# Packed diagonal maxima, exponent floors on ScalarE and unread transposes at the end of a fused attention and FP4 layer

## The chip, the cores and the metric

The kernel runs on one core of a Trainium2 chip. The metric is the device time of one execution in microseconds. The engines are PE (TensorE), DVE (VectorE), ACT (ScalarE), POOL (GpSimd) and SP (SyncE, which only issues transfers here).

## What is computed

One block adds two branches to its input of 2048 rows of 128. `_layernorm` takes away the mean and divides by the deviation.

```python
x = L0_attn_hidden_states                      # (1, 2048, 128)
xn = _layernorm(x, axis=-1)
x = x + _L0_attn_ref(xn, w_attn, b_attn, w_proj, b_proj) + _L0_ffn_ref(xn, w_gate, w_up, w_down)
...
# attention: 16 heads of 8
scores = jnp.einsum('bhqd,bhkd->bhqk', q, k) * scaling
scores = scores + _power_law_mask(S, scores.dtype)[None, None]   # -log(distance + 1), one side only
attn = jax.nn.softmax(scores, axis=-1)
out = jnp.einsum('bhqk,bhkd->bhqd', attn, v)
...
# FFN, inner width 352; every operand is first put through blocks of 16 on the FP4 grid
scale = jnp.maximum(jnp.max(jnp.abs(xb), axis=-1, keepdims=True) / 6.0, 1e-12)
q = _GRID[jnp.searchsorted(_MID, jnp.abs(xb / scale))] * jnp.sign(xb / scale) * scale
h = jax.nn.silu(fp4_linear(x, w_gate)) * fp4_linear(x, w_up)
return fp4_linear(h, w_down)
```

A query sees the keys from its own place on, so only one triangle of the 2048 x 2048 scores is used.

## The kernel before

**Units.** The attention works in 16 units: four groups of 512 queries (`GROUPS`, in the order 3, 2, 0, 1) by four sets of four heads. Each unit has two parts.

**Maxima.** First come the row maxima. For each of four blocks of 128 queries (`a`), each of four heads (`j`) and each group of 512 keys (`c`) from the unit's own on, PE multiplies queries by keys into one bank of PSUM (L1354). For the unit's own group (`c == g`) only the 512 - 128a keys from the block's own on are needed, and a second matmul adds the triangular mask (L1357). DVE then takes the maximum of the bank's columns into one column of `mxp` (L1135). Two closing reduces over `mxp` (item `parts`, L1146 and L1151) make the negated maxima, POOL splits them into three bfloat16 parts (item `minor`), PE turns them (item `rows`), and a transfer sets them into rows of `qop`, so that the next product subtracts them by itself.

**Steps.** Then come the steps, 160 over all units, each one block of 128 keys for the four heads. PE multiplies keys by queries (item `st`, L1378, with the mask at L1381 on the diagonal), ACT takes the exponential (L954), the result is multiplied by the distance weights, and PE multiplies by the values (item `pv`, L1396, one step is four matmuls in the program and eight records in the trace). Weighing is done for two heads at once by POOL (L802) from a ring of eight slots, or for one head by DVE straight from PSUM (L1162). After a unit's last step ACT copies the sums (item `evac`, L979), PE turns them (`close`, L1404), DVE divides (`norm`), and after four units PE turns the result (`turn`, L1412), ACT adds a bias (L973) and PE projects (`project`, L1419).

**FFN.** Sixteen tiles of 128 rows run beside this. PE makes gate and up (item `gu`), ACT copies and makes the curves (`curve`, L922 to L931), DVE works through the nine `silu` stages (L1097 to L1121): the product, the maximum of each block of 16, the scale, the scaled values, and then the rounding unit. That is the exponent's bits by themselves (L1117) and `max(e, 1) * ROUND` (L1121). POOL rounds by adding and taking away this unit and multiplies by the scale (item `quant`, L818, L820, L822), PE turns the tile (`hT`) and multiplies it by the down weights (`down`). The input and the weights go through the same rounding early, in six pieces (item `fp4`, L1041 to L1058 on DVE, then L782 to L789 on POOL).

**Order.** `plan()` simulates the engines with costs of its own and writes each engine's list of items; `build()` issues them in that order, so on the chip each engine's order is fixed. On PE a `max` item has rank 4 while DVE has fewer than two of them ahead and rank 7 after that, `st` has 4.5. On DVE a `max` item has rank 4 while the maxima are behind a curve of needed lead, and otherwise 7, behind the weighing at 5. The planner gives a pair of heads to DVE where POOL's queue is behind by more than a limit:

```python
behind = max(clock["POOL"], now) + waiting["POOL"] - now
pair_vec[p] = behind > (LAST_QUEUE if work["max"] == total else POOL_QUEUE)
```

The first limit, 1500, holds once all the maxima are done, 3800 before. `FILL` items of PE, transposes into a bank that nobody reads (L1244), stand early in the program.

## Time and profile before

| | |
|---|---|
| median of 3 runs | 627.31 us (627.09 to 627.82) |
| the profiled execution's own time | 626.35 us |
| its span in the profile | 624.5 us |
| busy: PE, DVE, ACT, POOL | 564.4, 562.8, 400.8, 537.4 us |
| share of the span | 90%, 90%, 64%, 86% |

The span runs from the first instruction to the last; some microseconds of the execution lie outside it. A matmul's end is modelled, so PE's busy time holds the time that a result needs to come out of the array. An engine's busy time counts overlapping instructions once.

### The profile page before, as it was taken

How to read it: one execution, taken by the hardware profiler on the slowest of the kernel's cores; microseconds unless marked ns; L12 is line 12 of the kernel's file. 1: busy time of each engine (PE TensorE's matmuls, PEld its weight loads, DVE VectorE, ACT ScalarE, POOL GpSimd, SP SyncE). 2: the span in 40 equal slices, each digit the busy share in tenths (PEclk: the TensorE clock that was granted, in tenths of full speed). 3: DMA queues.
4: the chain of work that ended last, by engine and by line, in shares of the span. 5: the costliest groups of instructions: out<-in, count | busy, mean ns of one | idle time of the engine just before them, and what ended most of it. 6: DMA issues, size and time to landing. Idle time of an engine off the chain costs nothing.

```text
span 624.5 us, 11270 instructions
## 1 busy us (share of the span) xinstructions
PE 564.4 (90%) x3807; PEld 250.9 (40%) x3807; DVE 562.8 (90%) x1178; ACT 400.8 (64%) x857; POOL 537.4 (86%) x400
## 2 busy tenths in 40 slices
PE   6999779999999999999989899999989898989985
PEld 5576534444343334333333332342334242432322
DVE  6899998989999999999999999998989999997661
ACT  4576457566656475767667577666656667759782
POOL 7226987789899989999998999999998999998992
PEclk9999988999999999999999999999999999999997
DMA  5255341310000000200000000000000000000000
GB/s 148 74 137 114 119 83 51 78 43 36 2 2 3 0 2 10 86 1 2 2 0 2 19 1 1 2 2 1 1 2 1 19 0 2 1 2 1 1 2 17
DMA packets 14715, 16.66 MB, mean 27 GB/s; under 512 B 1594, under 2 KB 14171, under 8 KB 14243
## 3 DMA queue, kind: packets, MB, share of 16 engines
q1 hardware_dynamic: 14123, 15.70, 9.2%
q8 instruction: 30, 0.49, 0.3%
q10 hardware_dynamic: 536, 0.26, 0.2%
q14 instruction: 26, 0.21, 0.1%
HBM read 11.75 MB, written 4.01 MB: 25 GB/s over the span
## 4 chain that ended last, share of the span: by engine, by line
PE 43%; POOL 32%; DVE 13%; ACT 7%; issue 4%; ACTq 0%; POOLq 0%; DVEq 0%
POOL ring L802 25%; PE psum L1396 11%; PE psum L1354 9%; PE psum L1378 7%; DVE mxp L1135 7%; ACT ring L954 2%; POOL xw L820 2%; POOL xw L818 2%; PE psum L1331 2%; POOL xw L822 2%; PE psum L1312 2%; PE psum L1314 1%; PE psum L1320 1%; DVE ring L1162 1%; PE psum L1404 1%
## 5 line engine op out<-in xcount | busy, mean ns | idle before, releaser
L802 POOL TENSOR_TENSOR ring<-ring,dist 128x1024 f32<-128x1024 f32 (+3 forms) x223 | 438.4, 1996 | 31.7 <-ACT ring L954 31.3
L1135 DVE TENSOR_REDUCE mxp<-psum 128x1 f32<-128x512 f32 (+3 forms) x640 | 352.6, 598 | 20.5 <-PE psum L1354 11.4
L954 ACT ACTIVATE ring<-psum 128x512 f32<-128x512 f32 (+3 forms) x446 | 211.5, 528 | 101.5 <-PE psum L1381 51.9
L1354 PE MATMUL psum<-kop,qop 96*128 96x512 bf16 (+3 forms) x640 | 198.0, 352 | 7.3 <-DVE mxp L1135 5.3
L1378 PE MATMUL psum<-qop,kop 128*128 128x512 bf16 (+3 forms) x640 | 190.7, 349 | 6.2 <-DVE mxp L1135 3.7
L1396 PE MATMUL psum<-ring,vaug 128*32 128x512 f32 (+3 forms) x1280 | 151.5, 544 | 15.0 <-POOL ring L802 14.1
L1162 DVE TENSOR_TENSOR ring<-psum,dist 128x512 f32<-128x512 f32 (+3 forms) x194 | 115.7, 622 | 13.9 <-ACT psum L954 13.8
L954 ACT ACTIVATE psum<-psum 128x512 f32<-128x512 f32 (+3 forms) x194 | 99.5, 543 | 39.7 <-PE psum L1378 23.4
L1354 PEld LDWEIGHTS psum<-kop,qop 96*128 96x128 bf16 x640 | 57.2, 97 | 127.8 <-DVE mxp L1135 46.5
L1378 PEld LDWEIGHTS psum<-qop,kop 128*128 128x128 bf16 x640 | 59.7, 97 | 82.2 <-DVE mxp L1135 15.5
L1357 PE MATMUL psum<-tri_q,identb 128*128 128x128 bf16 x256 | 56.2, 221 | 0.0
L1381 PE MATMUL psum<-tri_k,identb 128*128 128x128 bf16 x256 | 52.3, 219 | 0.0
L1396 PEld LDWEIGHTS psum<-ring,vaug 128*32 128x32 f32 x1280 | 26.7, 108 | 61.0 <-issue 59.9
L1357 PEld LDWEIGHTS psum<-tri_q,identb 128*128 128x128 bf16 x256 | 25.2, 99 | 12.2 <-issue 1.1
L1244 PE MATMUL psum<-identf 128*128 128x128 f32 x200 | 29.9, 274 | 0.0
L1381 PEld LDWEIGHTS psum<-tri_k,identb 128*128 128x128 bf16 x256 | 25.1, 98 | 7.9 <-issue 0.3
L1244 PEld LDWEIGHTS psum<-identf 128*128 128x128 f32 x200 | 22.1, 141 | 2.0 <-issue 0.5
L922 ACT ACTIVATE xw<-psum 128x352 f32<-128x352 f32 x16 | 7.4, 464 | 22.4 <-PE psum L1314 22.4
L807 POOL TENSOR_TENSOR mres<-mneg,mpart 128x16 f32<-128x16 f32 x16 | 3.6, 227 | 20.4 <-DVE mpart L1151 20.4
L782 POOL TENSOR_TENSOR xw<-xw,hT 128x512 f32<-128x512 f32 (+1 forms) x6 | 7.8, 1304 | 10.4 <-DVE hT L1058 10.4
L1331 PE MATMUL psum<-wdT,hT 128*128 128x128 f32 (+1 forms) x96 | 14.9, 291 | 1.4 <-ACT hT L940 1.2
L820 POOL TENSOR_TENSOR xw<-xw 128x352 f32<-128x352 f32 x16 | 14.9, 931 | 1.3
(130 smaller groups left out, 490.2 us busy)
## 6 DMA issues: line engine op xcount, KB each, us to landing
kop<-parts_dram SPq DMA_DIRECT2D x9, 384.0 KB
qop<-parts_dram SPq DMA_DIRECT2D x9, 384.0 KB
parts_dram<-qpart SPq DMA_DIRECT2D x18, 128.0 KB, 2.8
xin<-_attn_hidden_states_dram SPq DMA_DIRECT2D x4, 256.0 KB, 4.7
ring<-inv_dram SPq DMA_DIRECT2D x1, 1024.0 KB, 4.9
out_dram<-xin SPq DMA_DIRECT2D x4, 256.0 KB, 2.3
parts_dram<-qpart SPq DMA_DIRECT2D x6, 96.0 KB
qop<-parts_dram SPq DMA_DIRECT2D x3, 192.0 KB
```

The lines of the kernel that those rows point to most:

```text
L802: g_.tensor_tensor(slot(p)[:, :, 0:n], slot(p)[:, :, 0:n], both, ALU.mult).then_inc(weighed_pool, 1)
L820: g_.tensor_tensor(v, v, c, ALU.subtract).then_inc(hq_seq, 1)
L954: a_.activation(scores if pair_vec[p] else slot(p)[:, e % 2, 0:n], scores, ACT.Exp, scale=SCALE).then_inc(exp_done, 1)
L1135: v_.tensor_reduce(mxp[:, u % 2, 4 * a + j, c - g:c - g + 1], bank(*o)[:, 0:n], AX_X, ALU.max).then_inc(max_used, 1)
L1162: v_.tensor_tensor(slot(p)[:, e % 2, 0:n], bank("st", e)[:, 0:n], weights(d, n), ALU.mult).then_inc(weighed_vec, 1)
L1244: nc.tensor.transpose(psum[:, OUT_BANK, 0:P], identf[:], identf[:])
L1331: ins = mm(down_of(i), hT[0:k, i % 2, m], wdT[0:k, m], start=(m == 0), stop=(m == 2))
L1354: ins = mm(bank(*o)[:, 0:n], qop[0:K_MAX, u // NQ % 2, h, P * a:P * (a + 1)], kop[0:K_MAX, h, k0:k0 + n], start=True, stop=(c != g))
L1357: ins = mm(bank(*o)[:, 0:P], identb[:], tri_q[:], start=False, stop=True)
L1378: ins = mm(bank(*o)[:, 0:n], kop[0:K_ST, h, P * b:P * (b + 1)], qop[0:K_ST, u // NQ % 2, h, 0:n], start=True, stop=(d >= TPG))
L1381: ins = mm(bank(*o)[:, P * d:P * (d + 1)], identb[:], tri_k[:], start=False, stop=True)
L1396: ins = mm(psum[32 * j:32 * j + 32, OUT_BANK, 0:n], vaug[:, b, VC * h:VC * h + 32], slot(2 * s + j // 2)[:, j % 2, 0:n], start=(b == NT - ...
```

## The change

**Packed maxima.** In a unit's own key group, the bank of block 0 stays as it was. Block 1 (384 keys) and block 3 (128 keys) of one head now share a bank, and block 2 (256 keys) of two heads share one. One DVE reduce takes four maxima of 128 columns each from such a bank. Over a unit that is 10 banks in place of 16; the matmuls are the same in number and columns, each with its mask. `mxp` has three more columns per row (`NMX`), and its rows stand in the order 0, 2, 1, 3 (`ROW_OF`), so that four results lie side by side. The closing reduces read all seven columns, and where the next unit but one has fewer key groups, a memset clears the last of them.

**Floors on ACT.** `max(e, 1) * ROUND` becomes `Relu(ROUND * e - ROUND) + ROUND`: two passes of ACT with bias operands from `rounds`, for the 16 tiles (item `floor`) and the six pieces (item `floor4`). DVE has a stage fewer in both, and POOL waits for ACT in place of DVE.

**Unread transposes.** After the last `pv` PE may take 24 `tail` items, transposes of the identity into a free bank, at the lowest rank.

```diff
-SILU_STAGES, FP4_STAGES = 9, 6
+SILU_STAGES, FP4_STAGES = 8, 5
+NMX = NG + 3
+ROW_OF = [0, 2, 1, 3]
+TAIL = 24
...
+def max_pieces(a, j):
+    if a == 1:
+        return [(1, j), (3, j)]
+    if a == 2:
+        return [(2, j), (2, j + 1)] if j % 2 == 0 else []
+    return [(0, j)] if a == 0 else []
...
+    for k in range(TAIL):
+        pe(("tail", k), 2 * P, [], rank=9)
...
+        act(("floor4", n), GQ, [("DVE", ("fp4", n, FP4_STAGES - 1))], n=2, rank=3)
...
-                    pe(item, n + (P if c == g else 0), needs, rank=6)
-                    vec(item, n, [("PE", item)], rank=6)
+                    pe(item, GQ + (P * len(pieces) if c == g else 0), needs, rank=6)
+                    vec(item, GQ, [("PE", item)], rank=6)
...
-        pool(("quant", i), 2700, [("DVE", ("silu", i, SILU_STAGES - 1))], rank=0)
+        act(("floor", i), F, [("DVE", ("silu", i, SILU_STAGES - 1))], n=2, rank=2)
+        pool(("quant", i), 2700, [("ACT", ("floor", i))], rank=0)
...
+            if kind == "tail" and ("PE", ("pv", len(steps) - 1)) not in seen:
+                return None
...
-            work["max"] += TPG - item[2] if item[4] == units[item[1]][0] else TPG
+            work["max"] += TPG
...
+                if o[0] == "floor":
+                    i = o[1]
+                    act.wait_ge(silu_seq, SILU_STAGES * (i + 1))
+                    a_.activation(fbuf[:, 1], gate_of(i), ACT.Relu, scale=ROUND, bias=rounds[:, 0:1]).then_inc(floor_seq, 1)
+                    act.wait_ge(floor_seq, i + 1)
+                    a_.activation(fbuf[:, 1], fbuf[:, 1], ACT.Identity, bias=rounds[:, 1:2]).then_inc(fround_ready, 1)
...
-                    else:
-                        v_.tensor_scalar(c, gate, 1.0, ROUND, ALU.max, ALU.mult).then_inc(fround_ready, 1)
+                    ins.then_inc(silu_seq, 1)
...
-                    v_.tensor_reduce(mxp[:, u % 2, 4 * a + j, c - g:c - g + 1], bank(*o)[:, 0:n],
-                                     AX_X, ALU.max).then_inc(max_used, 1)
+                    if c == g and a:
...
+                        parts = bank(*o).rearrange("p (b n) -> p b n", n=P)
...
+                        v_.tensor_reduce(into, parts, AX_X, ALU.max).then_inc(max_used, 1)
...
-                        v_.tensor_reduce(mpart[:, s, :, 0], mxp[:, s, :, 0:nc_].rearrange("p (a j) c -> p a j c", j=4),
+                        v_.tensor_reduce(mpart[:, s, :, 0].rearrange("p a j -> p j a"), mxp[:, s],
                                          AX_X, ALU.max, negate=True).then_inc(mneg_ready, 1)
+                        if u + 2 < len(units) and parts_of(u + 2)[2] < parts_of(u)[2]:
+                            vec.wait_ge(mneg_ready, 2 * u + 2)
+                            v_.memset(mxp[:, s, :, :, NG - 1:NG], NEG)
...
+                if o[0] == "tail":
+                    bank_free(*o)
+                    nc.tensor.transpose(bank(*o)[:, 0:P], identf[:], identf[:])
...
-                    ins = mm(bank(*o)[:, 0:n], qop[0:K_MAX, u // NQ % 2, h, P * a:P * (a + 1)],
-                             kop[0:K_MAX, h, k0:k0 + n], start=True, stop=(c != g))
-                    if c == g:
-                        ins = mm(bank(*o)[:, 0:P], identb[:], tri_q[:], start=False, stop=True)
+                    for b, jj in max_pieces(a, j) if c == g else [(a, j)]:
...
```

The planner runs with these items, so the lists of all engines are written anew. On PE, around the last of the maxima (L1354 before, L1412 in the changed kernel, `kop,qop`; `qop,kop` is a step's score product, `ring,vaug` a step's value product, `wgT` and `wuT` the gate and up products of an FFN tile), the program stood so before, two units from its end:

```order
L1354 MATMUL psum<-kop,qop 128x512
L1378 MATMUL psum<-qop,kop 128x512
L1396 MATMUL psum<-ring,vaug 32x128 x4
L1354 MATMUL psum<-kop,qop 128x512
L1378 MATMUL psum<-qop,kop 128x512 x3
L1404 MATMUL psum<-identf,osb 128x128 x4
L1378 MATMUL psum<-qop,kop 128x512
L1396 MATMUL psum<-ring,vaug 32x512 x4
L1378 MATMUL psum<-qop,kop 128x512 x3
```

and the changed kernel has there:

```order
L1412 MATMUL psum<-kop,qop 128x512
L1437 MATMUL psum<-qop,kop 128x512 x2
L1412 MATMUL psum<-kop,qop 128x512
L1437 MATMUL psum<-qop,kop 128x512
L1455 MATMUL psum<-ring,vaug 32x384 x4
L1368 MATMUL psum<-wgT,xnT 128x352
L1370 MATMUL psum<-wuT,xnT 128x352
L1437 MATMUL psum<-qop,kop 128x512 x2
L1455 MATMUL psum<-ring,vaug 32x256 x4
L1437 MATMUL psum<-qop,kop 128x512
L1455 MATMUL psum<-ring,vaug 32x128 x4
L1424 MATMUL psum<-identb,mpart 12x128 x4
```

Before, 136 of the 160 value products stand ahead of the last of these maxima and 24 behind it; in the changed kernel 121 stand ahead and 39 behind, the first three of them the short last steps of a fourth unit.

At the end of the program PE had, from the last two value products on:

```order
L1396 MATMUL psum<-ring,vaug 32x256 x4
L1396 MATMUL psum<-ring,vaug 32x128 x4
L1404 MATMUL psum<-identf,osb 128x128 x4
L1412 MATMUL psum<-identf,xw 128x128 x4
L1419 MATMUL psum<-wp,xw 128x128 x4
```

and the changed kernel has:

```order
L1455 MATMUL psum<-ring,vaug 32x256 x4
L1455 MATMUL psum<-ring,vaug 32x128 x4
L1298 MATMUL psum<-identf 128x128 x8
L1463 MATMUL psum<-identf,osb 128x128 x4
L1298 MATMUL psum<-identf 128x128 x8
L1471 MATMUL psum<-identf,xw 128x128 x4
L1298 MATMUL psum<-identf 128x128 x8
L1478 MATMUL psum<-wp,xw 128x128 x4
```

The eight-fold rows of L1298 are the unread transposes; each group stands ahead of a turn or product whose input another engine still makes.

On ACT, ahead of the copies of an FFN tile's turned result (`hT<-psum`) in the middle of the program, there stood only exponentials (L954):

```order
L954 ACTIVATE psum<-psum 128x512
L954 ACTIVATE ring<-psum 128x512 x6
L954 ACTIVATE psum<-psum 128x512 x2
L954 ACTIVATE ring<-psum 128x512 x4
L954 ACTIVATE psum<-psum 128x512 x3
L937 ACTIVATE hT<-psum 128x256
L940 ACTIVATE hT<-psum 96x128
```

and the changed kernel has, with exponentials at L995:

```order
L995 ACTIVATE psum<-psum 128x512
L995 ACTIVATE ring<-psum 128x512 x8
L995 ACTIVATE psum<-psum 128x512
L970 ACTIVATE xw<-psum,rounds 128x352
L972 ACTIVATE xw<-xw,rounds 128x352
L995 ACTIVATE psum<-psum 128x512
L995 ACTIVATE ring<-psum 128x512 x2
L995 ACTIVATE psum<-psum 128x512 x2
L978 ACTIVATE hT<-psum 128x256
L981 ACTIVATE hT<-psum 96x128
```

The two floors (`rounds`) stand among the exponentials, three rows ahead of the copies that depend on them by way of POOL and PE.

## Rows read from the trace of the kernel before

**Rows 1.** Busy time by stretch: us, then per engine busy us (instructions), PEclk, DMA.

```profile
0.00:100.00 100.00, 84.29 (x606) 58.30 (x607) 87.78 (x214) 56.91 (x91) 57.92 (x93) 0.95 0.41 105
100.00:562.00 462.00, 429.25 (x2853) 174.48 (x2851) 440.36 (x897) 299.23 (x669) 433.25 (x281) 1.00 0.04 13
562.00:615.00 53.00, 47.07 (x336) 15.20 (x334) 33.47 (x65) 43.54 (x99) 46.27 (x28) 1.00 0.00 1
615.00:624.50 9.50, 3.76 (x16) 2.91 (x16) 1.24 (x3) 1.14 (x2) 0.00 (x0) 0.56 0.10 28
```

**Rows 2.** The same for the value product's matmuls (L1396) alone, on PE.

```profile
100.00:562.00 462.00, 123.08 (x1048) 21.77 (x1048) 1.00 0.04 13
562.00:615.00 53.00, 23.02 (x192) 4.10 (x192) 1.00 0.00 1
```

**Rows 3.** Groups by line and shape: count, busy us, mean ns, idle before.

```profile
L802 POOL TENSOR_TENSOR ring<-ring,dist 128x1024 f32<-128x1024 f32 x152 | 354.8, 2362 | 24.0 <-ACT ring L954 23.7
...
L1135 DVE TENSOR_REDUCE mxp<-psum 128x1 f32<-128x512 f32 x448 | 290.9, 679 | 14.6 <-PE psum L1354 11.4 <-PE psum L1357 2.1
...
L1162 DVE TENSOR_TENSOR ring<-psum,dist 128x512 f32<-128x512 f32 x144 | 94.6, 680 | 9.6 <-ACT psum L954 9.4
...
L802 POOL TENSOR_TENSOR ring<-ring,dist 128x768 f32<-128x768 f32 x21 | 38.0, 1816 | 3.7 <-ACT ring L954 3.7
...
L1135 DVE TENSOR_REDUCE mxp<-psum 128x1 f32<-128x128 f32 x64 | 17.2, 279 | 1.6 <-PE psum L1357 1.5
...
L1162 DVE TENSOR_TENSOR ring<-psum,dist 128x384 f32<-128x384 f32 x22 | 11.6, 547 | 1.7 <-ACT psum L954 1.7
...
L1107 DVE TENSOR_REDUCE psum<-xw 128x22 f32<-128x352 f32 x16 | 8.2, 514 | 0.0
...
L1121 DVE TENSOR_SCALAR xw<-psum 128x352 f32<-128x352 f32 x16 | 8.2, 511 | 0.0
```

**Rows 4.** Timeline, DVE, near 605 us: start, length of the run, count.

```profile
605.31 2.48 DVE L1162 TENSOR_TENSOR ring<-psum,dist 128x512 f32<-128x512 f32 x4 [0.68 <-ACT psum L954]
```

**Rows 5.** Groups of DVE: the fp4 floor; a unit's first closing reduce, two shapes.

```profile
L1058 DVE TENSOR_SCALAR hT<-hT 128x512 f32<-128x512 f32 (+1 forms) x6 | 3.8, 635 | 0.0
...
L1146 DVE TENSOR_REDUCE mneg<-mxp 128x16 f32<-128x64 f32 x4 | 0.8, 208 | 0.0
...
L1146 DVE TENSOR_REDUCE mneg<-mxp 128x16 f32<-128x16 f32 x4 | 0.7, 174 | 0.0
```

**Rows 6.** Groups of ACT: passes without and with a bias operand, and PSUM source.

```profile
L979 ACT ACTIVATE osb<-psum 128x512 f32<-128x512 f32 x16 | 9.6, 602 | 2.0 <-PE psum L1396 2.0
...
L929 ACT ACTIVATE xw<-xw 128x352 f32<-128x352 f32 x16 | 8.1, 507 | 0.0
...
L922 ACT ACTIVATE xw<-psum 128x352 f32<-128x352 f32 x16 | 7.4, 464 | 22.4 <-PE psum L1314 22.4
...
L973 ACT ACTIVATE xw<-psum,bv 128x512 f32<-128x512 f32 x4 | 2.8, 688 | 3.7 <-PE psum L1412 3.7
```

**Rows 7.** Waits of DVE: us in total, times, longest.

```profile
DVE mxp L1135 <- PE psum L1357: 8.0, 9, 1.5
```

**Rows 8.** Timeline, a gated tile: DVE's floor, then POOL's quantiser.

```profile
323.47 0.51 DVE L1121 TENSOR_SCALAR xw<-psum 128x352 f32<-128x352 f32 x1
...
324.38 0.93 POOL L818 TENSOR_TENSOR xw<-xw 128x352 f32<-128x352 f32 x1
```

**Rows 9.** Timeline, the end: PE's close, turn and projection.

```profile
615.60 0.63 PE L1404 MATMUL psum<-identf,osb 128*128 128x128 f32 x4 [0.80 <-ACT osb L979]
...
616.99 1.09 PE L1412 MATMUL psum<-identf,xw 128*128 128x128 f32 x4 [0.77 <-DVE xw L1176]
...
618.95 2.04 PE L1419 MATMUL psum<-wp,xw 128*128 128x128 f32 x8 [0.87 <-ACT xw L973]
```

**Rows 10.** Busy time by stretch at the end, columns as in rows 1.

```profile
616.00:617.00 1.00, 0.23 (x4) 0.04 (x1) 0.55 (x2) 0.00 (x0) 0.00 (x0) 0.61 0.00 0
617.00:618.00 1.00, 1.00 (x4) 0.68 (x4) 0.00 (x0) 0.00 (x0) 0.00 (x0) 0.50 0.00 0
```

More of the change, by code:

```diff
@@ L152, in plan @@
             needs += [("POOL", ("fp4", n - 1, 1))] if k == 4 and n else []
-            vec(("fp4", n, k), (GQ, 64, 150, GQ, GQ, GQ)[k], needs, rank=FP4_RANK)
+            vec(("fp4", n, k), (GQ, 64, 150, GQ, GQ)[k], needs, rank=FP4_RANK)
+        act(("floor4", n), GQ, [("DVE", ("fp4", n, FP4_STAGES - 1))], n=2, rank=3)
         for k in range(3):
             pool(("fp4", n, k), (1345, 1345, 1015)[k],
-                 [("POOL", ("fp4", n, k - 1)) if k else ("DVE", ("fp4", n, FP4_STAGES - 1))], rank=1)
+                 [("POOL", ("fp4", n, k - 1)) if k else ("ACT", ("floor4", n))], rank=1)
     for m in range(3):
@@ L168, in plan @@
                 for c in range(g, NG):
-                    n = GQ - P * a if c == g else GQ
+                    pieces = max_pieces(a, j) if c == g else [(a, j)]
+                    if not pieces:
+                        continue
                     item = ("max", u, a, j, c)
-                    h = 4 * hq + j
+                    h = 4 * hq + pieces[-1][1]
                     if g == GROUPS[0]:
@@ L266, in released @@
         kind = o[0]
-        by = {"xnT": ("ACT", o), "v": ("ACT", o), "dist": ("ACT", o), "wT": ("ACT", o), "xqT": ("ACT", o),
+        by = {"tail": ("PE", o), "xnT": ("ACT", o), "v": ("ACT", o), "dist": ("ACT", o), "wT": ("ACT", o), "xqT": ("ACT", o),
               "max": ("DVE", o), "rows": ("ACT", o), "close": ("DVE", ("norm",) + o[1:]), "turn": ("ACT", o),
@@ L393, in plan @@
     while True:
-        busy = [e for e in queues if any(left[e].get(k, 0) < len(q) for k, q in queues[e].items())]
+        busy = [e for e in queues if any(k != "tail" and left[e].get(k, 0) < len(q) for k, q in queues[e].items())]
         if not busy:
@@ L931, in _ @@
                     a_.activation(fbuf[:, 3], fbuf[:, 3], ACT.Exp, scale=-1.0).then_inc(curve_ready, 1)
+                if o[0] == "floor4":
+                    n = o[1]
+                    c = qx[:, 0:PIECES[n][1]]
+                    if n == 0:
+                        act.wait_ge(rounds_ready, 2)
+                    act.wait_ge(fp4_scaled, FP4_STAGES * (n + 1))
+                    a_.activation(c, c, ACT.Relu, scale=ROUND, bias=rounds[:, 0:1]).then_inc(floor4_seq, 1)
+                    act.wait_ge(floor4_seq, n + 1)
+                    a_.activation(c, c, ACT.Identity, bias=rounds[:, 1:2]).then_inc(round_ready, 1)
+                if o[0] == "floor":
[4 more added lines that the diff above has]
+                    a_.activation(fbuf[:, 1], fbuf[:, 1], ACT.Identity, bias=rounds[:, 1:2]).then_inc(fround_ready, 1)
                 if o[0] == "hT":
```

53 lines of the change are left out of this document (37 added, 16 removed).

## The prediction

> **What bounds the kernel now.** I read the busy time by stage first. From 100 us to 562 us DVE is busy 440.4 of 462 us (95%) and POOL 433.3 (94%); PE shows 429.3, with modelled ends, and ACT only 299.2 (65%) [rows 1]. DVE and POOL are one pair: both weigh exponentials by distance, POOL two heads in one pass of 2.36 us, DVE one head in 0.68 us, and the planner hands DVE whatever POOL's queue doesn't hold [rows 3]. DVE also does every maximum. The maxima end at 562 us; from there to 615 us DVE falls to 33.5 of 53 us while POOL keeps 46.3 and ACT rises to 43.5 [rows 1]. The pace tells the same: a step of the value product is 8 records of L1396, so the middle does 131 steps in 462 us (3.53 us each) and the last stage 24 in 53 us (2.21 us) [rows 2]. So there are two stages with different limits: DVE with POOL up to the last maximum, then exponentials, POOL and the loop between them. What is left, 9.5 us, is a serial end [rows 1].
>
> **Packed maxima.** Columns stay: 10 reduces of 512 in place of 16 of 512, 384, 256 and 128, four heads each, are 5,120 columns a unit both ways. What goes is six starts a unit, 96 in all. A start alone is 0.279 - 128 x 1.042 = 0.145 us (slope from 0.679 and 0.279) [rows 3]. But in series it is less: four operations of 512 columns took 2.48 us, so (2.48 - 0.68) / 3 = 0.60 us each, 0.08 less than one alone [rows 4]. So a start in series is 0.065 us, and 96 are **-6.2 us** of DVE (upper bound 13.9, none of them in series). Several results from one bank have no row; the nearest, L1107, makes 22 results of 352 columns in 0.514 us, where L1121 passes the same columns in 0.511 [rows 3], so the extra lies between nothing and 0.003 us, and I take nothing. The Trainium skill, VectorE: DVE Perf Modes, section on the TRN2 errata, gives a fixed term of about 150 cycles (0.156 us) for each instruction; by it the packing would be worth 15 us, by the row in series 6. The trace agrees for an instruction alone and not in series, so the sum goes by the row.
>
> **Maxima of maxima.** The two closing reduces of a unit now read 112 elements in place of 16 to 64. From 0.174 us at 16 to 0.208 at 64 [rows 5], 112 costs 0.24, 0.06 over the mean: 32 times, **+1.9 us**. Two small memsets are under 0.4 us.
>
> **Floors on ACT.** DVE loses L1121, 16 times 0.511 - 0.08 = 0.43 us [rows 3], and L1058, 3.8 us in six [rows 5], 3.3 in series: -6.9 and **-3.3 us**. ACT gains two passes for each: a pass with a bias operand took 0.688 against 0.602 us without [rows 6], so a 352-column floor is about 0.46 + 0.09 and 0.51 + 0.09, 1.15 us, some 0.95 in series; 16 are 15 us, and six of 512 columns another 7 us, 22 us on an engine with a third of the middle free. It is also a new wait: ACT stands for the seventh DVE stage, and behind it stand exponentials, which feed POOL; POOL's quantiser then stands for ACT. Its cover: at the seventh tile L1121 ended at 323.98 us and POOL came to the quantiser at 324.38, since it was still weighing [rows 8]. 0.4 us of cover against some 0.7 us of added path (1.15 for 0.43) would leave POOL idle for 0.3 us; POOL's own backlog is one pair or more nearly everywhere, and a stalled pass is made up from it later, so I take nothing, with 16 x 0.3 = 5 us as the bound.
>
> **What moves.** The order of the changed kernel has 121 value steps ahead of the last maximum and 39 behind it, where before had 136 and 24: with DVE lighter the planner lets the maxima run ahead. DVE then has 124 heads to weigh ahead of that point, not 146 (20 fewer of 512 and two of 384 columns: -20 x 0.60 - 2 x 0.47 = **-12.9 us**), and 13 tiles of the gated layer, not 15: 15 x 7 stages of 0.43 to 13 x 6 of 0.43, **-11.6 us**, L1121's share in it. Over the whole run only two pairs of 384 columns leave POOL, 2 x 1.82 = 3.6 us [rows 3].
>
> **The sum.** First stage: DVE is busy 87.8 + 440.4 = 528.2 us up to 562. Off it go 6.2 + 3.3 + 12.9 + 11.6 - 1.9 = 32.1 us, at 95% busy 33.7 us of time. DVE also waited 8.0 us on the matmul that masks a diagonal bank [rows 7], largely short fills, which the packing thins; I take a quarter, 2 us. The last maximum comes at 526 us. Second stage: in blocks of 128 keys by 128 queries the 24 steps were 84 (two units of 42), the 39 are three units and the 6 blocks that end a fourth, 132. 53 us x 132 / 84 = 83.3, less 2.3, as the run-out at the very end (some 4 us) comes once; plus 1.5 tiles of the gated layer over their share (2.5 us of ACT each) and three floors, 6.6 us of ACT, of which I count half, since ACT was 82% busy there: 84.3 us. The end: 24 unread transposes in three groups of eight. The clock fell to 0.61 of full between 616 and 617 us, the level of 1.2 GHz following, after PE had stood idle for the evacuation; the transposes of L1412 then took 1.09 us for four and the projection 2.04 us [rows 9, 10]. At the full 2.4 GHz four transposes were 0.63 us (L1404, at 615.60) [rows 9], so the two could give back 0.46 and about 0.95 us. Against it stands that the eight are queued ahead of the close, of the turn and of the projection: by L1404's four in 0.63 us, a run-out included, eight are 0.9 to 1.2 us, in gaps of 0.77 to 0.87 us, some 0.2 us late each time. **-0.7 us**, 8.8 us. Sum 526 + 84.3 + 8.8 = 619.1 us of span, against 624.5. The profiled execution took 626.35, 1.85 more than its span, and the median shown is 627.31, 0.96 above that. So 619.1 + 1.85 + 0.96 = **622 us**, a gain of 5.4 us. Of some 14.5 us taken off DVE most is spent in a longer last stage, where DVE isn't the limit.
>
> **The rivals.** A measurement of this kernel tells 0.2% (1.25 us) from no change.
> *All of the relief arrives.* DVE and POOL even out on the chip, and starts cost nearer 0.145 than 0.065. DVE is 14.5 us lighter; sharing x us of POOL's work for 0.51x of DVE's (1.20 for 2.36) evens at 14.5 / 1.51 = 9.6 us, and with half of the masked waits gone 13: **614 us**. For it: both engines are 95% busy; against it: the order as built moves 3.6 us off POOL.
> *The stages cancel.* The masked waits stay, so the first stage is 528 us, and the last keeps 2.21 us a step, 39 x 2.21 = 86 us, with a third of the 6.6 us of ACT 88: 528 + 88 + 8.8 + 2.8 = 628 us, no change. For it: a step's pace in the last stage is the only rate there that rows show.
> *Slower: ACT becomes the limit.* In the last stage ACT would have 43.5 x 132 / 84 + 6.6 = 75 us to do; if its 82% is the most that the loop allows, that is 91.5 us, 7 more than I count, 629 us, and a part of the 5 us that floors can cost POOL makes it **630 us**. It decides from a last stage over 91 us. For it: ACT is busy 43.5 of 53 there and waits in order. The Trainium skill, ScalarE: Activation LUTs, Rules for kernel authors, speaks for this one: it sends relu, add and multiply to VectorE, not ScalarE. No row here has those operations on ACT beside DVE, but the pass with a bias at 0.688 us shows the price; against the rule, ACT has the idle time in the middle.
> *The end* can cost instead: if the clock falls all the same, 8 transposes take twice as long and two groups come some 0.9 us late, +1.8 us; it shifts each case and decides none.
>
> **How the numbers follow.** Forecast 0.41, with 618 to 626 as its own range; all of the relief 0.22; cancel 0.13; ACT the limit 0.24. Faster by over 0.2% is the first two, 0.63; same 0.13; slower 0.24. Half of the second and less than half of the last lie outside 612 to 632, under 2 in 10.
>
> **What would show it.** Right: the maxima number 544, cost 0.60 us each in series, and DVE's total falls by about 11 us net of weighing; the last maximum stands at 520 to 530 us; the rest up to the last value product takes 82 to 87 us with DVE under 65% busy; POOL's wait for ACT ahead of the quantiser stays under 4 us in all; the turn takes under 0.7 us at full clock. Wrong: a last maximum after 535 us (the first stage isn't DVE's), a last stage over 91 us (ACT) or under 78 us (the exponentials had room), POOL's wait at the quantiser over 8 us, or reduces with four results dearer than 0.60 us.

## Result, and the profile after

The changed kernel takes 637.3 us (four runs, 634.9 to 640.1), the kernel before 627.2 in the same comparison: a ratio of 1.0163, with a 95% interval of 1.0111 to 1.0214. It is slower by about 10 us; 622 us was forecast, and the range ended at 632. Two of the four runs took 634.9 and 635.5 us at a mean granted clock of 0.986, the other two 639.1 and 640.1 us at 0.975; the profiled execution is the fastest of them, 634.91 us with a span of 633.1.

Busy time by stretch of the changed kernel, cut at its own last maximum and last value product; the columns are those of [rows 1].

```profile
0.00:100.00 100.00, 77.64 (x580) 57.01 (x581) 79.28 (x175) 57.04 (x87) 50.81 (x91) 0.95 0.39 105
100.00:533.00 433.00, 401.67 (x2668) 167.75 (x2667) 412.64 (x780) 288.67 (x640) 405.20 (x263) 0.99 0.04 13
533.00:624.50 91.50, 76.37 (x543) 26.43 (x544) 56.46 (x110) 76.27 (x172) 76.94 (x47) 1.00 0.00 1
624.50:633.10 8.60, 5.11 (x48) 4.54 (x48) 1.24 (x3) 1.28 (x2) 0.00 (x0) 0.95 0.11 32
```

Added up and set against [rows 1], DVE does 549.6 us and not 562.8, ACT 423.3 and not 400.8, POOL 533.0 and not 537.4. So the relief was real, and the time rose all the same. In the first 100 us DVE is busy 8.5 us less than before, POOL 7.1 and PE 6.7; where they stood is shown below. The last stage is 91.5 us for 39 value steps.

The groups that answer to [rows 3, 5, 6]: maxima with one result and with four, the two closing reduces, and ACT's two passes for a tile's floor.

```profile
L1184 DVE TENSOR_REDUCE mxp<-psum 128x1 f32<-128x512 f32 x448 | 287.0, 677 | 17.7 <-PE psum L1415 8.9 <-PE psum L1412 8.1
...
L1182 DVE TENSOR_REDUCE mxp<-psum 128x4 f32<-128x512 f32 x96 | 63.8, 678 | 5.6 <-PE psum L1415 5.6
...
L1199 DVE TENSOR_REDUCE mpart<-mxp 128x16 bf16<-128x112 f32 x16 | 4.2, 262 | 0.0
L1194 DVE TENSOR_REDUCE mneg<-mxp 128x16 f32<-128x112 f32 x16 | 4.1, 255 | 0.1
```

```profile
L972 ACT ACTIVATE xw<-xw,rounds 128x352 f32<-128x352 f32 x16 | 9.4, 588 | 0.5
L970 ACT ACTIVATE xw<-psum,rounds 128x352 f32<-128x352 f32 x16 | 8.9, 555 | 3.1 <-DVE psum L1155 3.0
```

Four results from a bank cost what one does (678 and 677 ns), and a floor on ACT costs 0.555 + 0.588 = 1.14 us. These pieces cost what the prediction said.

Where the engines stood still is seen in the timeline of PE, between a score block at 70.74 us and the first maximum of unit 4 (the first of the second group of queries):

```profile
70.63 0.27 PE L1437 MATMUL psum<-qop,kop 128*128 128x256 bf16 x1
70.74 0.22 PE L1440 MATMUL psum<-tri_k,identb 128*128 128x128 bf16 x1
...
79.11 0.61 PE L1412 MATMUL psum<-kop,qop 96*128 96x512 bf16 x1 [8.15 <-DMA qop<-parts_dram]
```

The chain of the same stretch says why: POOL's last pass on the second chunk's parts, the transfer out, then the queries coming back.

```profile
50.93 1.17 POOL qpart L801
52.11 2.29 DMA parts_dram<-qpart
...
58.53 20.53 DMA qop<-parts_dram
79.06 0.05 issue
79.11 0.61 PE psum L1412
```

PE takes its list in order. It came to a maximum whose queries landed at 79.06 us, 27 us after POOL's pass ended at 52.10: 2.3 us for the way out, 4.1 in which SyncE issued six transfers back (three of keys, three of queries), 20.5 until the last of them had landed. The planner's table (DMA_CHUNK, line 75) puts 17 us there. While PE stood, nothing behind it could start: score blocks, exponentials and the banks that DVE reduces. The ten microseconds from 70 to 80, in the columns of rows 1:

```profile
60.00:70.00 10.00, 9.80 (x80) 7.37 (x81) 9.93 (x17) 8.01 (x19) 6.84 (x7) 1.00 0.54 141
70.00:80.00 10.00, 1.85 (x13) 1.17 (x12) 2.25 (x7) 2.38 (x7) 7.02 (x8) 0.79 0.30 111
80.00:90.00 10.00, 10.00 (x77) 6.68 (x76) 8.70 (x16) 4.32 (x11) 4.20 (x3) 0.87 0.61 120
```

PE is busy for 1.85 of those 10 us and DVE for 2.25. In the kernel before, DVE was still reducing unit 3 when the queries came; its last of those, and its first of unit 4, on DVE:

```profile
80.31 0.28 DVE L1135 TENSOR_REDUCE mxp<-psum 128x1 f32<-128x128 f32 x1
...
81.06 0.68 DVE L1135 TENSOR_REDUCE mxp<-psum 128x1 f32<-128x512 f32 x1
```

On PE the first value step stood ahead of unit 4's first maximum there:

```profile
76.43 1.51 PE L1396 MATMUL psum<-ring,vaug 128*32 128x512 f32 x8
...
78.29 0.61 PE L1354 MATMUL psum<-kop,qop 96*128 96x512 bf16 x1
```

In the changed kernel the first value step stands behind nine banks of unit 4's maxima, which PE goes through from 79.11 us on:

```profile
87.33 1.07 PE L1455 MATMUL psum<-ring,vaug 128*32 128x512 f32 x8
```

So the transfer had been hidden by the very work that the packing made cheaper, and only just: e4 below, with the maxima unpacked, waits 0.7 us at that place.

The starts of some value steps (first of a step's eight records) and of the last maximum tell how far each run is; the experiments below are read with the same table. A row is one profiled execution; the times given as measured are medians of 5 to 12 runs. All in us.

| kernel | step 0 | step 24 | step 124 | step 159 | last maximum | span | 0 to 159 |
|---|---|---|---|---|---|---|---|
| before | 76.4 | 168.0 | 520.8 | 614.4 | 561.7 | 624.5 | 538.0 |
| changed | 87.3 | 180.6 | 538.5 | 624.5 | 532.5 | 633.1 | 537.2 |
| e1 late q | 77.1 | 167.5 | 523.8 | 613.3 | 532.2 | 621.9 | 536.2 |
| e2 packed only | 87.3 | 173.2 | 531.6 | 622.4 | 550.0 | 632.4 | 535.1 |
| e3 floors only | 84.9 | 169.3 | 527.5 | 622.9 | 566.2 | 632.9 | 538.0 |
| e4 tails only | 77.8 | 170.1 | 522.6 | 616.2 | 563.6 | 624.9 | 538.4 |
| e5 no floors, late q | 77.9 | 167.6 | 527.8 | 613.9 | 545.3 | 622.5 | 536.0 |
| e6 held maxima | 78.3 | 171.3 | 527.0 | 626.5 | 586.5 | 635.2 | 548.2 |
| e8 before, tails, late q | 77.1 | 169.7 | 522.2 | 615.8 | 563.2 | 624.5 | 538.7 |
| e12 tile floors only | 77.2 | 165.7 | 528.2 | 628.0 | 553.1 | 637.6 | 550.8 |
| e16 queue 3000 | 80.0 | 169.7 | 529.5 | 622.0 | 548.1 | 630.6 | 542.0 |

The changed kernel reaches step 0 10.9 us late; from there to step 159 it needs 537.2 us, as long as before (538.0). The whole loss is there ahead of step 0; the relief after it brought 0.8 us, and the end is 1.5 us shorter.

### The profile page after: what moved, and what is told of

Its sections match the earlier page's. It is cut to its first block, busy times and chain, and to the rows that moved or that the text cites. A ratio compares the mean times of both kernels' runs of the same rounds, so it can differ in the third digit from the quotient of the medians.

```text
span 633.1 us, 11248 instructions
## 1 busy us (share of the span) xinstructions
PE 560.8 (89%) x3831; PEld 255.7 (40%) x3831; DVE 549.6 (87%) x1066; ACT 423.3 (67%) x901; POOL 533.0 (84%) x400
## 4 chain that ended last, share of the span: by engine, by line
PE 39%; POOL 39%; DVE 7%; ACT 6%; issue 4%; DMA 4%; SPq 1%; ACTq 0%; POOLq 0%; DVEq 0%
POOL ring L828 31%; PE psum L1455 10%; PE psum L1412 8%; PE psum L1437 7%; DMA qop<-parts_dram 3%; DVE mxp L1184 2%; ACT ring L995 2%; POOL xw L846 2%; PE psum L1387 2%; POOL xw L844 2%; POOL xw L848 2%; PE psum L1368 1%; ACT psum L995 1%; PE psum L1463 1%; PE psum L1370 1%
## 5 line engine op out<-in xcount | busy, mean ns | idle before, releaser
L1184 DVE TENSOR_REDUCE mxp<-psum 128x1 f32<-128x512 f32 x448 | 287.0, 677 | 17.7 <-PE psum L1415 8.9
L995 ACT ACTIVATE ring<-psum 128x512 f32<-128x512 f32 (+3 forms) x442 | 209.3, 528 | 98.8 <-PE psum L1440 52.9
L1412 PE MATMUL psum<-kop,qop 96*128 96x512 bf16 (+3 forms) x640 | 191.4, 352 | 11.9 <-DMA qop<-parts_dram 8.1
L1437 PE MATMUL psum<-qop,kop 128*128 128x512 bf16 (+3 forms) x640 | 186.2, 349 | 4.9 <-DVE ring L1213 1.5
L1213 DVE TENSOR_TENSOR ring<-psum,dist 128x512 f32<-128x512 f32 (+3 forms) x198 | 117.7, 621 | 28.5 <-ACT psum L995 27.9
L995 ACT ACTIVATE psum<-psum 128x512 f32<-128x512 f32 (+3 forms) x198 | 100.9, 543 | 33.4 <-PE psum L1440 21.0
L1412 PEld LDWEIGHTS psum<-kop,qop 96*128 96x128 bf16 x640 | 57.6, 98 | 119.9 <-DVE mxp L1184 36.6
L1182 DVE TENSOR_REDUCE mxp<-psum 128x4 f32<-128x512 f32 x96 | 63.8, 678 | 5.6 <-PE psum L1415 5.6
L1415 PE MATMUL psum<-tri_q,identb 128*128 128x128 bf16 x256 | 48.2, 221 | 0.0
L1440 PEld LDWEIGHTS psum<-tri_k,identb 128*128 128x128 bf16 x256 | 25.2, 98 | 10.2 <-issue 0.7
L808 POOL TENSOR_TENSOR xw<-xw,hT 128x512 f32<-128x512 f32 (+1 forms) x6 | 7.9, 1311 | 21.2 <-ACT hT L966 21.2
L1376 PE MATMUL psum<-identf,xw 128*128 128x128 f32 (+1 forms) x48 | 8.8, 291 | 12.0 <-POOL xw L848 11.8
```

The lines of the kernel that those rows point to most:

```text
L995: a_.activation(scores if pair_vec[p] else slot(p)[:, e % 2, 0:n], scores, ACT.Exp, scale=SCALE).then_inc(exp_done, 1)
L1182: v_.tensor_reduce(into, parts, AX_X, ALU.max).then_inc(max_used, 1)
L1184: v_.tensor_reduce(mxp[:, u % 2, j, ROW_OF[a], c - g:c - g + 1], bank(*o), AX_X, ALU.max).then_inc(max_used, 1)
L1213: v_.tensor_tensor(slot(p)[:, e % 2, 0:n], bank("st", e)[:, 0:n], weights(d, n), ALU.mult).then_inc(weighed_vec, 1)
L1412: ins = mm(bank(*o)[:, x0:x0 + n], qop[0:K_MAX, u // NQ % 2, 4 * hq + jj, P * b:P * (b + 1)], kop[0:K_MAX, 4 * hq + jj, k0:k0 + n], start= ...
L1415: ins = mm(bank(*o)[:, x0:x0 + P], identb[:], tri_q[:], start=False, stop=True)
```

## Experiments

The theory (A) was that PE's wait for the second transfer makes the loss; against it stood that the floors on ScalarE slow the start (B) and that the longer last stage, paced by ScalarE, makes it (C).

**e1, the transfer told as it is.** One number of the planner's table:

```diff
+DMA_SECOND = 26000
...
-seen[("DMA", ("k", ci))] = end + DMA_CHUNK
+seen[("DMA", ("k", ci))] = end + (DMA_SECOND if ci == 1 else DMA_CHUNK)
...
-seen[("DMA", ("q", gi))] = end + DMA_CHUNK
+seen[("DMA", ("q", gi))] = end + DMA_SECOND
```

> The changed kernel, with the order's table told that the second transfer of keys and queries takes 26 us and not 17 us, so that TensorE's list has unit 4's maxima behind the first value steps and not ahead of them (20 score blocks before them, was 11). Theory A (8 us of the loss is TensorE standing before unit 4's first maximum until that transfer lands): the 8.1 us wait at that line is under 1 us, the first value step comes 7 to 9 us earlier than 87.3 us, and the time is 628 to 631 us. Rival B (the start is slow because of the floors on ScalarE or the quantiser's chain): the first value step stays after 84 us and the time within 2 us of the changed kernel's. Rival C (the loss is in the later stages; the start is caught up): the first value step comes early, but the time stays at 634 us or more.

Measured: 624.3 us (before 627.8; ratio 0.996, 0.994 to 0.998), 13 us under the changed kernel. The list of PE's waits from 60 to 95 us no longer names the transfer:

```profile
PE psum L1456 <- POOL ring L829: 3.1, 2, 2.4
PE psum L1307 <- DVE mxp L1185: 2.2, 1, 2.2
PE psum L1317 <- ACT xnT L883: 1.5, 1, 1.5
```

Step 0 starts 10.2 us earlier, step 159 11.2 us earlier. The wait that A named is gone, but its 628 to 631 us were missed on the fast side: the price was more than the 8.1 us of the wait. The edit does two things, for in this list step 0 (77.1 us) stands ahead of unit 4's first maximum (79.2 us) again. How the 10.2 us split between the wait and that place in the list was not measured.

**e2, packing alone.** Both kinds of floors back on DVE, no transposes at the end:

```diff
-SILU_STAGES, FP4_STAGES = 8, 5
+SILU_STAGES, FP4_STAGES = 9, 6
...
-TAIL = 24
+TAIL = 0
...
```

> The kernel before with the packed maxima alone: both kinds of floors on VectorE as before, no transposes at the end. In its list too TensorE reaches unit 4's first maximum ahead of the first value step (14 score blocks before it; the kernel before has 16 and the first value step). Theory A (packing runs ahead of the transfer of queries): a wait of 6 to 9 us at unit 4's first maximum, and a time of 630 to 636 us, slower than before. Rival B (the floors make the loss): no slower than before, 618 to 627 us. Rival C (a longer last stage makes the loss, since ScalarE's added 22 us set its pace): the last stage runs at 2.2 us for a value step as before, and the time is 622 to 628 us.

Measured: 635.4 us (1.011, 1.009 to 1.013). Of PE's waits over the whole run these two are on transfers:

```profile
PE psum L1416 <- DMA qop<-parts_dram: 4.1, 1, 4.1
...
PE psum L1416 <- DMA kop<-parts_dram: 2.6, 1, 2.6
```

The 4.1 us stand at unit 4's first maximum (78.18 us); A had 6 to 9 there. The 2.6 us stand at 48.02 us and belong to the first transfer; e1 waits 1.4 us there. Step 0 comes at 87.3 us as in the changed kernel, for half of its wait, and here too it stands behind unit 4's maxima, eleven banks of them. So packing alone meets the transfer, and what it costs is that wait together with the list behind it. B falls as the sole cause.

**e3, floors alone.** In the kernel before, both kinds of floors move to ScalarE, as the change does it; of the tiles' floors:

```diff
-SILU_STAGES, FP4_STAGES = 9, 6
+SILU_STAGES, FP4_STAGES = 8, 5
...
-v_.tensor_scalar(c, gate, 1.0, ROUND, ALU.max, ALU.mult).then_inc(fround_ready, 1)
...
+a_.activation(fbuf[:, 1], gate_of(i), ACT.Relu, scale=ROUND, bias=rounds[:, 0:1])
+a_.activation(fbuf[:, 1], fbuf[:, 1], ACT.Identity, bias=rounds[:, 1:2]).then_inc(fround_ready, 1)
```

> The kernel before with both kinds of floors on ScalarE alone: maxima unpacked, no transposes at the end. Theory A: the maxima aren't cheaper, so the list doesn't run ahead, and the wait for the queries is under 2 us; what is left is 1 to 2 us at the start (two more ScalarE passes in the chain to the quantised weights) and 10 us less of VectorE: 625 to 630 us. Rival B (the floors make the loss): 632 to 638 us. Rival C (ScalarE sets the pace of the last stage): the stages up to the last maximum as before, the last stage 2.35 us for a value step instead of 2.2, 628 to 632 us.

Measured: 631.9 us (1.008, 1.005 to 1.010). No wait for a transfer, as A had it, but the time missed A's 625 to 630: step 0 is 8.5 us late for another reason, and the rest takes 538.0 us, exactly as before. So C has no part in it. ACT's timeline shows what lies in the start: the pieces' floors, and a fill of the key rows.

```profile
49.32 0.72 ACT L946 ACTIVATE hT<-hT,rounds 128x512 f32<-128x512 f32 x1 [1.06 <-DVE hT L1077]
50.08 0.72 ACT L948 ACTIVATE hT<-hT,rounds 128x512 f32<-128x512 f32 x1
...
57.84 3.71 ACT L846 ACTIVATE kop<-krow 128x4096 f32<-128x4096 f32 x1
...
62.40 0.77 ACT L946 ACTIVATE hT<-hT,rounds 128x560 f32<-128x560 f32 x1
```

That fill stood at 51.29 us in the kernel before. Coming 6.5 us later can't be the reason by itself: e5 below has it at 57.84 us too, and its step 0 at 77.9. The second piece's floor stands behind the fill here, and GpSimd waits for it:

```profile
POOL xw L790 <- ACT hT L948: 15.3, 3, 7.7
```

The longest of these, 7.7 us, ends at 64.04 us; in the kernel before, GpSimd waited 5.2 us for this piece's floor on VectorE and went on at 59.19. Whether that makes the 8.5 us isn't shown. e1 carries the same floors and has step 0 at 77.1, so floors do not cost this in every order.

**e4, the closing transposes alone.**

```diff
+for k in range(TAIL):
+    pe(("tail", k), 2 * P, [], rank=9)
...
```

> The kernel before with only the 24 unread transposes behind the last value step. All theories: orders up to the last value step as before; the granted clock in the last 9 us rises from about 0.56 to 0.9 or more, the closing matmuls and turns take half as long, and the end is 0.7 to 1.0 us shorter: 626.2 to 626.7 us. The rival for this part: the transposes stand ahead of the closing matmuls in TensorE's list and lengthen the end: 627.3 us or more.

Measured: 625.4 us (0.997, 0.996 to 0.998), some 2 us and a little more than expected. In the traces the end, from the start of step 159, is 8.7 us and not 10.1: 1.4 us, twice the prediction's 0.7. The rest of the 2 us has no place in these two traces.

**e5, packing and closing transposes with the transfer told as 26 us.** e1 with both kinds of floors back on DVE:

```diff
-SILU_STAGES, FP4_STAGES = 8, 5
+SILU_STAGES, FP4_STAGES = 9, 6
...
```

> Packed maxima and the closing transposes with the floors on VectorE as before, and the second transfer told as 26 us in the order's table (the run that was slow with packing alone, 635.4 us, plus these two). Theory A (the transfer's wait at the start is what made packing slow): the first value step at 76 to 80 us, against 87.3 with packing alone, and 621 to 626 us. If the floors on ScalarE are worth something by themselves, this comes out above 624.3 us, the time of the same table with the floors on ScalarE; if they cost something, below. Rival (packing costs in the later stages): 630 us or more.

Measured: 623.9 us (0.994, 0.992 to 0.996). Packing alone, slow in e2, is fast with the wait gone: step 0 comes 9.4 us earlier than there. Beside e1's 624.3, floors on ScalarE are worth nothing that shows. The Trainium skill, ScalarE: Activation LUTs, Rules for kernel authors, keeps relu, add and multiply on VectorE; these two runs, 0.5 us apart, speak neither for it nor against it.

**e6, the maxima held back**, so that DVE keeps them for the last stage:

```diff
-return 4 if work["max"] < lead_at(work["st"]) else 7
+past = work["max"] - lead_at(work["st"])
+return 4 if past < 0 else 7 if past < 16 else None
```

> The changed kernel with the second transfer told as 26 us, and with the order held from taking a maximum more than 16 pieces ahead of its line: 141 value steps stand ahead of the last maximum (127 without the hold). Theory C (VectorE's gain is lost because the maxima run ahead and leave a last stage in which VectorE idles): VectorE busier in the end, and 617 to 622 us. Rival D (from the first value step on VectorE, GpSimd and TensorE are all over 90% busy, so where the maxima stand hardly matters): 623 to 626 us, as without the hold. Rival E (the hold makes GpSimd weigh more, 227 pairs against 219, and GpSimd is the bound): 627 us or more.

Measured: 637.5 us (1.016, 1.014 to 1.019). Theory C in this form fell: the last maximum comes at 586.5 us, only 19 value steps are behind it, and the run is 13 us slower than without the hold. Rival E's time came, but its bound is not shown by it: e13 below takes 20.8 us off GpSimd in e1's order for 1 us of time. Holding the maxima back helps nothing here; e1, whose maxima run ahead clear of the transfer, is the faster kernel.

**e7, less GpSimd work in the last stage.**

```diff
-POOL_QUEUE, LAST_QUEUE = 3800, 1500
+POOL_QUEUE, LAST_QUEUE = 3800, 500
```

> The changed kernel with the second transfer told as 26 us, and from the last maximum on 8 pairs of 31 fewer weighed by GpSimd (the table's queue of the last stage 500 instead of 1500): some 17 us less GpSimd work and 10.5 us more VectorE work behind the last maximum; the order up to there is the same. Theory P (GpSimd, 83% busy in the last stage, sets its pace): the last stage shrinks by 5 to 12 us, and the time is 612 to 620 us. Theory L (ScalarE and the loop through it set the pace): the last stage stays at 79 to 83 us, and the time is 623 to 626 us.

Measured: 624.2 us, e1's time. Busy time from 541 to 613 us (columns of rows 1), of e1 and then of e7:

```profile
541.00:613.00 72.00, 62.22 (x436) 21.09 (x442) 42.92 (x82) 58.98 (x135) 58.71 (x35) 0.98 0.00 1
```

```profile
541.00:613.00 72.00, 62.38 (x434) 21.11 (x434) 49.75 (x98) 58.49 (x135) 45.15 (x26) 0.98 0.00 1
```

POOL is 13.6 us lighter there, and steps 128 to 159 take 72.7 us, where e1 took 72.1. VectorE took 6.8 us more in exchange. POOL alone does not set that pace; theory L's time came.

**e8, a control:** the kernel before with the closing transposes (e4's edit) and the table's number:

```diff
+DMA_SECOND = 26000
...
```

> Control: the kernel before with the closing transposes, and the second transfer told as 26 us. Its maxima of unit 4 come as late as they did (three places behind in TensorE's list), so nothing waits less: 625 to 626 us, as with the transposes alone. If the table's number is worth something by itself, whatever the packing, it comes below 624 us.

Measured: 626.2 us (0.999, 0.997 to 1.000), as e4. The number by itself is worth nothing where the maxima don't run ahead. From e8 to e5, with packing, it is some 2.3 us; that compares two orders, and another order of e1's work lies 7 us from e1 (e16), so it isn't shown as the worth of packing.

That left a question: why does 13 us less on an engine that is 95% busy bring 2 us? Six of the next seven kernels, all but e12, take work off one engine (e15 off two) in e1's order, by leaving a part out.

**e9, VectorE lighter.** 76 of its multiplications do half of their columns:

```diff
+if 112 <= e < 496 and n == GQ:
+    n = GQ // 2
 v_.tensor_tensor(slot(p)[:, e % 2, 0:n], bank("st", e)[:, 0:n], weights(d, n),
```

> The changed kernel with the second transfer told as 26 us, in which 76 of VectorE's 202 multiplications by distance (512 columns wide, in steps 28 to 123) do only 256 columns: the other half of those weights is not multiplied, so the result is another. The order is the same. It takes 20.7 us (76 times the 0.273 us between 0.686 and 0.413) off VectorE ahead of the last maximum. Theory V (VectorE bounds the first stage, 96% busy): the last maximum comes 15 to 21 us earlier than 532.2 us and the time is 604 to 610 us. Theory S (GpSimd at 95% and TensorE at 93% are as full in that order, so VectorE's time is covered): the last maximum moves by 0 to 6 us, and the time is 618 to 625 us.

Measured: 625.0 us; the last maximum at 532.0 us (532.2 in e1). That is theory S: VectorE's time is covered by other engines.

**e10 and e11, the last stage with half of the value product, and with half of the exponentials.**

```diff
+n = n // 2 if s >= 128 else n
```

```diff
+if e // 4 >= 128:
+    n = n // 2
+    scores = bank(*o)[:, 0:n]
```

> The changed kernel with the second transfer told as 26 us, in which the value matmuls of steps 128 to 159 do only half of their columns (the other half of those sums is left out, so the result is another). The order is the same; TensorE has some 12 us less to do behind step 128 (72 us in the trace). Theory T (TensorE sets the pace of the last stage): the last stage is 8 to 13 us shorter, 611 to 617 us. Theory A (ScalarE sets it) and theory L (the loop of score, exponential, weight and value): 0 to 4 us shorter, 620 to 625 us.

> The changed kernel with the second transfer told as 26 us, in which the exponentials of steps 128 to 159 do only half of their columns (the rest keeps what stood there, so the result is another). The order is the same; ScalarE has some 16 us less to do behind step 128 (about 80 exponentials of 512 columns by 0.2 us). Theory A (ScalarE sets the pace of the last stage): 10 to 16 us shorter, 608 to 614 us. Theory T (TensorE sets it): 0 to 3 us shorter, 621 to 625 us. Between the two, 614 to 621 us, both stand in a loop and each delays the other.

Measured: 624.3 and 623.9 us. Steps 128 to 159 take 70.0 and 70.6 us, 2.1 and 1.5 less than in e1. In e10 PE's busy time from 541 to 613 us falls by 5.5 us where 12 were meant, at a granted clock of 0.93 and not 0.98, so it tests TensorE less hard than it was to. Busy time of e11 in the same window:

```profile
541.00:613.00 72.00, 64.19 (x446) 21.41 (x446) 43.97 (x84) 39.87 (x137) 60.15 (x35) 0.98 0.00 1
```

ACT is 19.1 us lighter and the stage hardly shorter: the rival that ACT sets the pace of the last stage falls, in this order at least.

**e12, the tiles' floors alone.** In the kernel before, only the 16 tiles' floors move to ScalarE:

```diff
-SILU_STAGES, FP4_STAGES = 9, 6
+SILU_STAGES, FP4_STAGES = 8, 6
...
```

> The kernel before with only the floors of the 16 tiles on ScalarE; the floors of the pieces of weights and activations stay on VectorE. Both kinds together made 631.9 us with the first value step at 84.9 us. Theory A (what the floors cost is the start: the two passes on the pieces stand in the chain ahead of step 0 and re-order it): the first value step at 76 to 78 us and 625 to 629 us. Rival C (the 16 us of tile floors on ScalarE are what costs): the first value step at 76 to 78 us all the same, and 630 us or more.

Measured: 640.1 us (1.021, 1.019 to 1.022). Step 0 comes at 77.2 us, as both theories had it; then the steps take 550.8 us. The time is rival C's, but e1 has the same tile floors and takes 536.2 us for those steps. So it isn't ScalarE's added work as such. What is left is the order that the planner makes with it; which place in it costs the time wasn't found. It gives POOL 227 pairs, as e6, the other slow one, but e16 below is slow with 214.

**e13, e14 and e15, GpSimd, TensorE, and GpSimd with VectorE lighter ahead of the last maximum.** e13's edit, then e14's; e15 has those of e9 and e13.

```diff
+if 56 <= p < 248 and p % 5 == 0 and n == GQ:
+    n = GQ // 2
```

```diff
+n = n // 2 if 28 <= s < 124 and s % 2 == 0 and n == GQ and b != NT - 1 else n
```

> The changed kernel with the second transfer told as 26 us, in which 22 of GpSimd's pairs (512 columns wide, in steps 28 to 123) are multiplied by distance in half of their columns only: the rest of those weights is not multiplied, so the result is another. The order is the same. It takes 24 us (22 times the 1.10 us between 2.363 and 1.268) off GpSimd ahead of the last maximum. Theory G (GpSimd bounds the first stage, 95% busy): the last maximum comes 15 to 24 us earlier than 532.2 us, the time is 600 to 610 us. Theory S (several engines are equally full and the order is fixed): 0 to 6 us earlier, 618 to 625 us.

> The changed kernel with the second transfer told as 26 us, in which 33 value steps between 28 and 123 do half of their columns (the rest of those sums is left out, so the result is another). The order is the same. It takes some 16 us (33 times 0.5 us) off TensorE ahead of the last maximum. Theory T (TensorE bounds the first stage): the last maximum comes 11 to 16 us earlier, 608 to 614 us. Theory S: 0 to 4 us earlier, 620 to 625 us.

> Both cuts of VectorE's (20.7 us) and of GpSimd's (24 us) multiplications ahead of the last maximum, in the order of the changed kernel with the second transfer told as 26 us; the result is another as in those two. Theory G: as with GpSimd's cut alone. Theory S with these two engines as the full ones: much more than the sum of the two cuts alone, the last maximum 12 to 20 us earlier, 604 to 612 us. If TensorE is as full as both, little moves here too: 0 to 6 us, 618 to 625 us.

Measured: 623.4, 621.9 and 619.3 us. Busy time from 168 to 524 us of e1, e9, e13 and e15, in this order:

```profile
168.00:524.00 356.00, 331.55 (x2135) 132.76 (x2162) 344.55 (x648) 239.40 (x524) 338.16 (x210) 1.00 0.02 7
```

```profile
168.00:524.00 356.00, 332.86 (x2166) 133.17 (x2170) 329.00 (x651) 239.40 (x525) 339.06 (x210) 1.00 0.02 7
```

```profile
168.00:524.00 356.00, 332.95 (x2134) 132.15 (x2163) 345.96 (x653) 241.07 (x527) 317.32 (x211) 1.00 0.02 7
```

```profile
168.00:524.00 356.00, 331.68 (x2147) 133.24 (x2177) 331.49 (x656) 241.56 (x529) 319.36 (x212) 1.00 0.02 7
```

The third busy figure is DVE, the fifth POOL. Steps 24 to 124 take 356.3 us in e1; e7, e10 and e11, whose programs are e1's up to there, take 356.3, 358.0 and 358.1, so a difference under 2 us is within the spread. With DVE 15.6 us lighter they take 355.4, with POOL 20.8 lighter 354.1, with 33 value steps halved (PE 6.0 us lighter) 355.8, with DVE and POOL lighter together 352.0. DVE, POOL or PE made lighter alone moves this stage by no more than some 2 us, though two are 95 to 97% busy; even both of these at once give 4.3 us back, 5.0 in the medians. For e15 that is the last of the three expectations, and not theory S's 604 to 612. In the medians e14 is 2.4 us under e1; where that comes from these traces don't show.

**e16, another order.** The queue's bound in the table:

```diff
-POOL_QUEUE, LAST_QUEUE = 3800, 1500
+POOL_QUEUE, LAST_QUEUE = 3000, 1500
```

> The changed kernel with the second transfer told as 26 us and the table's bound on GpSimd's queue 3000 instead of 3800, so that the order gives GpSimd 214 pairs and not 219 (some 10 us less) and VectorE 10 more multiplications (6.5 us more): the result is the reference's. Theory G: 612 to 620 us. Theory S: 621 to 626 us, as before within the spread of orders.

Measured: 631.4 us (1.007, 1.004 to 1.009). Both missed: POOL is 10 us lighter than in e1 over the run (520.0 for 530.2) and the time is 7 us longer. Here the new order cost more than the relief that it was made for brought.

## Why the prediction was wrong

**Packed maxima, closing reduces, the tiles' floors: right.** 544 maxima, four results as cheap as one; a reduce of 112 elements 0.255 and 0.262 us where 0.24 was said; a tile's floor 1.14 where 1.15 was said; ACT 22.4 us heavier (22 said). POOL's waits from 80 us on name the pieces' quantiser (L808) and, once, the tiles' (L844):

```profile
POOL xw L808 <- ACT hT L966: 14.2, 2, 8.6
...
POOL mres L833 <- DVE mpart L1199: 1.6, 3, 1.0
POOL xw L844 <- ACT xw L972: 0.4, 1, 0.4
```

For the tiles it is 0.4 us, well under the 4 that the forecast allowed. For the pieces the forecast had a price on ACT and no wait; over the whole run POOL stood 21.2 us for their floors, where it stood 10.4 us for DVE's before. 8.6 us of it ends at 85.80 us, in the stretch in which PE stood. With the order mended it is 15.6 us in e1 and 10.1 in e5, whose floors are on DVE, and the two take the same time. DVE's total fell by 13.2 us where about 11 were said.

**"The last maximum comes at 526 us": wrong, 533.** DVE did 491.9 us up to there, 4.2 less than the forecast's 528.2 - 32.1 = 496.1. But it idled 20.7 of the first 100 us, not 12.2 [rows 1]. The first step that failed is the sum of the first stage, which turned DVE's lighter work into time at 95%. It read "the planner lets the maxima run ahead" and followed only what that does to the last stage; it has no term for what the maxima run into at the front, the transfer of unit 4's queries. e1 shows the size of the term, the wait and the list behind it together: 11.2 us in the trace, 13.0 in the medians.

**"At 95% busy 33.7 us of time": not borne out even without that wait.** e9 takes another 15.6 us off DVE in e1's order and the last maximum stays where it was. That DVE and POOL were both near full was read rightly from [rows 1]; that the pace is therefore DVE's was not shown by it. What remained of the relief was about 2.3 us (e8 to e5), if it is that and not the order. DVE and POOL together give 4.3 us for 31.9 us of work. The Trainium skill, Perfetto Trace Analysis, Identifying the Most-Contended Engine, has the engine with the highest occupancy optimized first; here that engine's time, cut by 15.6 us in place, bought 0.9 us in the stage, within the spread, and none in the run, so the measurement decides against it for this kernel in this order. What does set the pace, beyond that several engines wait for each other in written lists, stays open; PE, whose busy time e14 lowers by only 6.0 us, is the engine least tested.

**The last stage: 84.3 forecast, 91.5 measured** for the 39 steps, 2.35 us a step. This is the second step that failed: of the 14.0 us between the span that the sum gave (619.1) and the measured one (633.1), 7.0 lie ahead of the last maximum, 7.2 behind it, and the end is 0.2 shorter. The forecast's slower rival, ACT as the limit, had 91.5 us for it and decided from 91. Its number came and its mechanism did not: with 19.1 us less ACT (e11) the steps behind 128 took 70.6 and not 72.1 us, and POOL (e7) or the value product (e10) changed as little. That was tried in e1's order, not in the changed kernel's. The sum's rate for these steps was too small, and no single engine's load explains it. Against the kernel before it is no loss: the 10.9 us were lost ahead of step 0, and steps 0 to 159 took 537.2 us beside 538.0. It is gain that the forecast counted on and that did not come.

**The end: right in its mechanism, too small in size.** PE at the end of the changed kernel:

```profile
625.74 0.60 PE L1463 MATMUL psum<-identf,osb 128*128 128x128 f32 x4
...
627.05 0.62 PE L1471 MATMUL psum<-identf,xw 128*128 128x128 f32 x4
...
628.45 1.16 PE L1478 MATMUL psum<-wp,xw 128*128 128x128 f32 x8
```

The turn takes 0.62 and not 1.09 us, the projection 1.16 and not 2.04 [rows 9], at a granted clock of 0.95, nearly all of it at 2.4 GHz, where before it was 0.56, mostly at 1.2 [rows 1]. The 0.6 us that I set against it for the transposes ahead of each did not come: e4's end is 1.4 us shorter.

**The rivals.** That all relief arrives (614) and that the stages cancel (628) both took the start as given. The slower rival was on the right side for a wrong reason, and that its last stage of 91.5 us came to the tenth is luck.

## What to carry to other kernels

Where a static order is planned with assumed landing times, a faster engine runs its list ahead: list every transfer that the earlier work now meets, and read when it really lands (here 27 us after its source, with 17 in the table). A transfer that shows no wait before may be hidden by just the work that gets cheaper. And a busy share of 95% doesn't price a saving: cut that engine's work in the same order and see whether the end moves, before a new order is made for it.
